# Mixing attention values on 64 x 64 diagonal blocks, with accumulators by query halves

## Time and profile before

| | |
|---|---|
| median of three runs | 1387.43 us |
| the profiled execution | 1390.95 us |
| its span | 1389.2 us |
| TensorE matmul busy | 1332.2 us |
| VectorE busy | 900.5 us |
| ScalarE busy | 754.5 us |
| POOL busy | 682.5 us |
| mean granted TensorE clock | 0.991 |

### The profile page before, as it was taken

The page is one execution under the profiler, slowest core; times in us unless marked ns, Lnnn a source line. Parts: engine busy times, 40 slices in busy tenths (PEclk is TensorE's granted clock), DMA queues, the critical chain, the costliest instruction groups (busy, mean ns, idle before and its releaser), DMA issues.

```text
span 1389.2 us, 34054 instructions
## 1 busy us (share of the span) xinstructions
PE 1332.2 (96%) x12776; PEld 1037.0 (75%) x12776; DVE 900.5 (65%) x1496; ACT 754.5 (54%) x2685; POOL 682.5 (49%) x719
## 2 busy tenths in 40 slices
PE   6798888999999999999999999999999999999998
PEld 3586666877778777777778777787777877777776
DVE  6657774477755777457764677547775577745775
ACT  2346664266733666256662666526663366624665
POOL 5226553266541766236652465426654176623664
PEclk9899999999999999999999999999999999999999
DMA  6214441424322342323414144142432234231332
GB/s 236 67 63 134 125 124 54 138 74 116 103 86 82 97 125 87 112 69 100 132 58 142 49 111 132 32 137 76 123 95 91 77 101 122 85 114 54 100 102 60
DMA packets 71554, 138.35 MB, mean 100 GB/s; under 512 B 15328, under 2 KB 29152, under 8 KB 71136
## 3 DMA queue, kind: packets, MB, share of 16 engines
q1 hardware_dynamic: 70400, 135.46, 33.7%
q10 hardware_dynamic: 992, 0.73, 0.2%
HBM read 73.21 MB, written 12.58 MB: 62 GB/s over the span
## 4 chain that ended last, share of the span: by engine, by line
PE 79%; DVE 7%; POOL 5%; ACT 5%; issue 3%; DMA 1%; SPq 0%; DVEq 0%; POOLq 0%
PE PROJ L898 14%; PE PROJ L899 13%; PE PROJ L900 13%; PE O L1072 13%; PE S L1042 11%; PE TR L1053 8%; ACT e_sb L596 2%; POOL e_sb L488 2%; PE S L898 2%; PE S L899 2%; PE S L900 2%; DVE S L822 1%; DVE negmax L829 1%; POOL p_cur L496 1%; PE S L982 1%
## 5 line engine op out<-in xcount | busy, mean ns | idle before, releaser
L596 ACT ACTIVATE e_sb<-S,negmax 128x128 f32<-128x128 f32 x1024 | 362.4, 369 | 127.4 <-DVE negmax L829 126.4
L488 POOL TENSOR_TENSOR e_sb<-e_sb,rinv 128x512 f32<-128x512 f32 x256 | 266.0, 1039 | 287.9 <-DVE rinv L834 262.6
L712 DVE TENSOR_TENSOR prod<-PROJ,rope_sb 128x1024 f32<-128x1024 f32 x160 | 195.5, 1222 | 86.4 <-PE PROJ L900 85.3
L1042 PEld LDWEIGHTS S<-k_stack,q_stack 64*64 64x64 f32 x5632 | 171.3, 133 | 72.0 <-issue 39.0
L822 DVE COPY_PREDICATED S<-diagonal_key,S 128x512 f32<-128x512 int8 x192 | 133.1, 693 | 124.4 <-PE S L1042 124.0
L1042 PE MATMUL S<-k_stack,q_stack 64*64 64x64 f32 (+2 forms) x5632 | 213.2, 275 | 0.0
L596 ACT ACTIVATION_READ_ACCUMULATOR e_sb<-S,negmax 128x1 f32 x1024 | 211.7, 207 | 0.0
L606 ACT ACTIVATE pt_sb<-TR 128x512 f32<-128x512 f32 x256 | 153.7, 600 | 91.1 <-PE TR L1053 87.9
L496 POOL TENSOR_SCALAR_AFFINE_SELECT p_cur<-pt_sb 128x512 f32<-128x512 f32 x256 | 163.2, 638 | 51.9 <-ACT pt_sb L606 46.6
L1053 PE MATMUL TR<-ident,e_sb 128*128 128x128 f32 x1024 | 167.6, 286 | 21.1 <-POOL e_sb L488 16.4
L829 DVE TENSOR_REDUCE negmax<-S 128x4 f32<-128x512 f32 x256 | 177.0, 691 | 8.8
(11 more groups left out here) (96 smaller groups left out, 2609.4 us busy)
## 6 DMA issues: line engine op xcount, KB each, us to landing
q_stack<-qy SPq DMA_DIRECT2D x512, 64.0 KB, 2.0
wq_ring<-wq_split_d SPq DMA_DIRECT2D x56, 512.0 KB, 3.5
wo_ring<-wo_split_d SPq DMA_DIRECT2D x56, 512.0 KB, 3.3
k_stack<-ky SPq DMA_DIRECT2D x256, 64.0 KB, 2.1
x_in<-x SPq DMA_DIRECT2D x8, 512.0 KB, 4.1
wq_split_d<-wq_ring SPq DMA_DIRECT2D x8, 512.0 KB, 3.7
wo_split_d<-wo_ring SPq DMA_DIRECT2D x8, 512.0 KB, 3.6
out<-acc SPq DMA_DIRECT2D x8, 512.0 KB, 4.9
```

Of the source, the lines that this page charges most:

```text
L488: nc.gpsimd.tensor_tensor(e, e, r, ALU.mult).then_inc(norm_done, 1)
L596: last = nc.scalar.activation(e_sb[:, n % 2, r, :], s_heads(n, 1)[:, r, :], ACT.Exp, bias=negmax[:, n % 2, r:r + 1], accum_out=rowsum[:, n ...
L712: nc.vector.tensor_tensor(prod[:, 2 * part:2 * part + 2, :], both, rope_sb[:, :, :], ALU.mult).then_inc(prod_done, 1)
L1042: last = nc.tensor.matmul(dst[:, at:at + (blocks - 1) * step + 1:step, :], q_stack[rows, g % 2, slot, i * P + a * HP:i * P + (a + 1) * HP] ...
```

## The change

The mixing works by halves of the 128 queries (a = 0 and 1). For queries of the first half, only places k < 64 can be of tile i; for those of the second half, places k < 64 always are, and only the others can be of either. So the first part of a step multiplies all of P (pt_sb, no longer p_cur) with v[i-1] for a = 0, and for a = 1 with v_mix, whose lower 64 places are of v[i] and upper 64 of v[i-1]. The second part multiplies only the diagonal 64 x 64 blocks of p_cur with v_step, on 64 rows. For i = 0 the scores' own mask already made P right, so neither mask nor second part is needed.

Half a = 0 accumulates in O, half a = 1 in the first half of TR, the transposes' bank. So the mixing of a pair waits for the copy of the transposes made in the same slot, and the transposes of odd slots wait (tr_read) until VectorE has read the half in TR. They are moved behind the filler of their slot. ScalarE and VectorE read the accumulators in two instructions, the half in TR first, and VectorE does so ahead of the fold. VectorE builds v_mix by `value_mix` in slots 0, 2 and 4. The load of Silu's table moves from slot 31 to slot 34.

```diff
+        O_half = [O[:, 0:2 * P].rearrange("p (s m q) -> p s m q", s=2, m=2),
+                  TR[:, 0:2, :].rearrange("p s (m q) -> p s m q", m=2)]
...
-                    if n >= 2:
+                    if 2 <= n <= STEPS + 1 and (n - 2) % TT:
                         mask(n - 2)
...
                     act.wait_ge(pv_done, b * STEPS + 2 * pair + 2)
-                    nc.scalar.activation(o_p[0][:, :, i * P:(i + 2) * P],
-                                         O[:, :].rearrange("p (m q) -> p m q", m=2), ACT.Copy
-                                         ).then_inc(o_copied, 1)
+                    for a in (1, 0):
+                        nc.scalar.activation(o_half(0, i, a), O_half[a].rearrange("p s m q -> p m s q"), ACT.Copy
+                                             ).then_inc(o_copied, 1)
...
-                    if n == STEPS - 1 and b + 1 < BATCH:
+                    if n == LAST_SLOT and b + 1 < BATCH:
                         load_table(ACT.Silu)
...
-                dve.wait_ge(o_copied, (row * STEPS) // 2 + pair + 1)
-                low(o_p[1][:, :, i * P:(i + 2) * P], O[:, :].rearrange("p (m q) -> p m q", m=2),
-                    o_p[0][:, :, i * P:(i + 2) * P]).then_inc(o_split, 1)
+                for a, done in ((1, tr_read), (0, o_split)):
+                    dve.wait_ge(o_copied, row * STEPS + 2 * pair + 2 - a)
+                    low(o_half(1, i, a), O_half[a].rearrange("p s m q -> p m s q"), o_half(0, i, a)).then_inc(done, 1)
...
+                def value_mix(i):
+                    dve.wait_ge(v_done, b * TT + i + 1)
+                    HP = P // 2
+                    nc.vector.tensor_copy(v_mix[0:HP, i - 1, :], v_sb[0:HP, i, :])
+                    nc.vector.tensor_copy(v_mix[HP:P, i - 1, :], v_sb[HP:P, i - 1, :]).then_inc(v_mixed, 1)
...
                 for n in range(LAST_SLOT + 1):
-                    early = n % 2
-                    if 1 <= n <= STEPS and early:
-                        inverse_sum(n - 1)
-                    if n < STEPS:
-                        fold(n)
-                    if 1 <= n <= STEPS and not early:
+                    if 1 <= n <= STEPS and n % 2:
                         inverse_sum(n - 1)
                     if n >= 5 and n % 2:
                         o_low(b, (n - 5) // 2)
+                    if n < STEPS:
+                        fold(n)
+                    if 1 <= n <= STEPS and n % 2 == 0:
+                        inverse_sum(n - 1)
+                    if n in (0, 2, 4):
+                        value_mix(1 + n // 2)
...
                         pe.wait_ge(t_copied, b * STEPS + n)
+                    if n >= 3 and n % 2:
+                        pe.wait_ge(tr_read, (b * STEPS + n - 3) // 2 + 1)
...
+                def values_mixed(pair):
+                    HP = P // 2
+                    pe.wait_ge(t_copied, b * STEPS + min(2 * pair + 3, STEPS))
+                    pe.wait_ge(v_done, b * TT + min(2 * pair + 2, TT))
+                    pe.wait_ge(v_mixed, b * (TT - 1) + min(2 * pair + 1, TT - 1))
+                    if pair:
+                        pe.wait_ge(o_split, b * STEPS // 2 + pair)
+                    for s in range(2):
+                        g, i = divmod(2 * pair + s, TT)
+                        heads = slice(g * D, (g + 1) * D)
+                        for a in range(2):
+                            v = v_mix[:, i - 1, heads] if i and a else v_sb[:, max(i - 1, 0), heads]
+                            for odd in range(2):
+                                last = nc.tensor.matmul(O_half[a][odd * D:(odd + 1) * D, s, :, :], v,
+                                                        pt_sb[:, (2 * pair + s) % 4, odd:REP:2, a * HP:(a + 1) * HP],
+                                                        start=s == 0, stop=False)
+                    pe.wait_ge(v_stepped, b * (TT - 1) + min(2 * pair + 1, TT - 1))
+                    for s in range(2):
...
+                        if i:
+                            pe.wait_ge(p_masked, b * MASKS + masks_upto(2 * pair + s))
+                            for odd in range(2):
+                                for a in range(2):
+                                    half = slice(a * HP, (a + 1) * HP)
+                                    last = nc.tensor.matmul(O_half[a][odd * D:(odd + 1) * D, s, :, :],
+                                                            v_step[half, i - 1, heads], p_cur[half, (2 * pair + s) % 4, odd:REP:2, half],
+                                                            start=False, stop=s == 1)
+                    last.then_inc(pv_done, 2)
...
-                    if 2 <= n <= STEPS + 1:
+                    if 2 <= n <= STEPS + 1 and n % 2 == 0:
                         transposes(n - 2)
...
+                    if 2 <= n <= STEPS + 1 and n % 2:
+                        transposes(n - 2)
                     if n >= 4 and n % 2 == 0:
-                        values_mixed(n - 4)
-                        values_mixed(n - 3)
+                        values_mixed((n - 4) // 2)
```

More of the change, by code:

```diff
@@ L122, in place, with masks_upto @@
         return TURN[what] % 2, TURN[what] + 1
+    def masks_upto(n):
+        return n - n // TT
+    MASKS = masks_upto(STEPS - 1)
     def stacked(b, g, semaphores, each):
@@ L176, in attention_and_ffn_block @@
         v_step = sb("v_step", [P, TT - 1, NKV * D])
-        staging_rest = sb("staging_rest", [P, CT * 2 * F - (TT - 1) * NKV * D])
+        v_mix = sb("v_mix", [P, TT - 1, NKV * D])
+        staging_rest = sb("staging_rest", [P, CT * 2 * F - 2 * (TT - 1) * NKV * D])
         qy = sb("qy", [P, 2, 2, T])
@@ L205, in attention_and_ffn_block, with o_half @@
         O = ctx.enter_context(nc.psum_tensor("O", [P, 512], fp32))
+        O_half = [O[:, 0:2 * P].rearrange("p (s m q) -> p s m q", s=2, m=2),
+                  TR[:, 0:2, :].rearrange("p s (m q) -> p s m q", m=2)]
         PROJ = ctx.enter_context(nc.psum_tensor("PROJ", [P, 2, 512], fp32))
         S4 = S[:, :, :, :, :].rearrange("p a b h k -> p (a b) (h k)")
+        def o_half(part, i, a):
+            tokens = o_p[part][:, :, i * P:(i + 2) * P].rearrange("p m (s a q) -> p m s a q", s=2, a=2)
+            return tokens[:, :, :, a, :]
         def s_heads(n, which):
@@ L278, in attention_and_ffn_block @@
         v_stepped = sem("v_stepped")
+        v_mixed = sem("v_mixed")
         pv_done = sem("pv_done")
@@ L281, in attention_and_ffn_block @@
         o_split = sem("o_split")
+        tr_read = sem("tr_read")
         wo_added = sem("wo_added")
@@ L513, in _ @@
                 rotate(b, "q", 2)
-                for n in range(STEPS + 2):
+                for n in range(LAST_SLOT + 2):
                     if 1 <= n <= STEPS:
@@ L1054, in transposes @@
                     last.then_inc(t_ready, 1)
[L1056 to L1072, removed]
-                                                    v[:, g * D:(g + 1) * D], p[:, n % 4, odd:REP:2, :],
-                                                    start=term == 0, stop=term == len(terms) - 1)
-                    last.then_inc(pv_done, 1)
+                def values_mixed(pair):
[16 more added lines that the diff above has]
+                    for s in range(2):
+                        g, i = divmod(2 * pair + s, TT)
+                        heads = slice(g * D, (g + 1) * D)
+                        if i:
[7 more added lines that the diff above has]
+                    last.then_inc(pv_done, 2)
```

## The result

The changed kernel takes 1397.46 us (median of five runs, 1395.18 to 1400.03) against 1387.43 (1386.48 to 1390.48) of the kernel before on the same chip: ratio 1.0066, 95% interval 1.0044 to 1.0088. It is slower, by 0.66%; the forecast was 1389.7, no change. One execution in experiment 11, the profiled one, took 2551 us where the others took 1379; it is left out, and no rows of it are used.

What follows compares the result with a forecast made beforehand. TensorE, busy 96% of the span, was taken as the bound. Six middle rows -3.9, last row +4.1 and first row +2.1 made +2.3 on the profiled 1390.95; with the median 3.5 lower, 1389.7 us, range 1376 to 1403.

Steps and rivals of the forecast that it cites:

- part 1: Mixing on TensorE: cheaper products save 0.43 us per pair of steps with i > 0, 0.21 with i = 0.
- the rival of 1431: Each TensorE instruction has its own price, 0.36 to 0.48 us more a pair, giving 1431 us; chance 0.03.
- Five switches before, five after: TensorE's changes of tile shape, 0.16 us each, stay equal in number per pair; bounds 0 to +0.16, taken as 0.
- part 2: Even slots' transposes wait for ScalarE's copy of the odd slot's: 0.05 us lost for i > 0, 0.26 for i = 0.
- thin cover of 0.13: In even slots the Q block hides mixing's wait for ScalarE's copy of the transposes by only 0.13 us.
- ScalarE's second copy: Rival: mixing is held by ScalarE's copy of the even slot's transposes; 0.25 us later adds 14 us, 1404; chance 0.22.
- The 1397 that this rival gives: Half of the +14 us for a late ScalarE copy, with value_mix calls of 1.36 us (+6), was said to give 1397.
- part 3: VectorE's value_mix, three calls a row: 0.80 to 1.36 us each, taken as 0.85; slots 1 to 6 net -0.1 a row.
- part 4: Places lacking cover: slot 24 +1.1 a row, pair (30, 31) gains nothing, last row +4.1, first row +2.1 us.
- Six such slots at 0.6: First row: waits behind weight splits lose 1.6 us each where about 1.0 before; with three lesser slots, +4 us.
- the saving arrives: Rival: a quarter to a half of the products' 41 us saving is kept, giving 1369 to 1380; chance of faster 0.29.
- plain wait of 0.95 against 0.69: Even slots, i = 0: ScalarE's copy frees the transposes after 0.95 us, while TensorE would be there at 0.69.

Runs made afterwards that it cites:

- experiment 11: The kernel before, with ScalarE's weight-split halves ahead of the exponentials and odd slots' transposes in the middle of the odd filler; ratio 0.9925.
- experiment 4: The changed kernel with the odd slots' transposes moved from behind the filler block to its middle; 1382.38 us, ratio 0.9952.
- experiment 1: The kernel before with only the odd slots' transposes moved behind the filler block, mixing, masks and accumulators untouched; 1410.12 us, ratio 1.0155.
- experiment 3: The changed kernel without value_mix, reading v_sb in place of v_mix (wrong values, same products); 1387.45 us, ratio 0.9995.
- experiments 9 and 10: Kernel before and changed kernel, each with ScalarE's halves of the first row's weight splits issued early, ahead of the exponentials; 1374.03 and 1377.46 us.

## Why the forecast was right or wrong

*Products (part 1): right.* 30 us left TensorE's busy time. Without the wait (experiment 4) a pair gains 0.39 and 0.15 against the forecast's 0.43 and 0.21. No price of an instruction shows: the rival of 1431 is dead. By the page "TensorEngine Tiling (Array Packing)" of the Trainium skill (Performance Considerations) the added matmuls would have taken back an estimated 0.3 to 0.4 a pair, if its overhead comes on top of each one's columns; the pairs disagree, with 0.04 and 0.06 missing. "Five switches before, five after" held within the same 0.04 to 0.06.

*The new wait (part 2): right.* Pairs of 7.14 and 6.91 against 7.13 and 6.91, 56 waits with 0.18 at i = 0, and experiment 1 shows the same wait without the products. Mixing's thin cover of 0.13 held: no wait of it in slots 16 to 19, so the rival "ScalarE's second copy" did not happen there: a steady row has two such waits, in slot 24 and at its end. The first row has ten (3.4 us). The 1397 that this rival gives with slow copies of the values is a wrong sum (1389.7 + 7 + 6 is 1403), and that the result lies beside it is chance. The read of TR was covered by 1.2 us, as worked out (1.1 against 2.2).

*value_mix (part 3): mis-sized.* "I take 0.85" a call; it measures 0.573 + 0.809 = 1.38 in the mean, just above the upper bound of 1.36, since half of its passes run beside POOL's. Its cost is 1.15 a row by removal (experiment 3), not the 0.2 that the sum held. The value was chosen by the look of a row with one tensor read, and not by what POOL does in those slots. A second error hides most of the first: with the copies gone, slots 0 to 7 take 23.92, 0.97 less than in the kernel before, where the forecast had 0.33. It is not the order (experiment 1 has 24.95 there). The traces point at the masks that POOL no longer makes for i = 0, which the forecast priced at nothing: in experiment 1, with the new order and all masks, a mask of 0.63 stands ahead of the scaling for slot 4, which starts 10.2 after the row's first scores, and that slot's mixing waits 0.42 for POOL's p_cur; in experiment 3 the scaling starts at 9.6, and there is no such wait. No run leaves out the masks alone, so this is a reading. The two leave +0.29 instead of -0.1, and rows 2 to 7 at -1.6 instead of -3.9. By the page "VectorE: DVE Perf Modes" of the Trainium skill (Mode 2x_2P) a call was an estimated 0.86; its 0.43 a copy agrees with the 0.41 of a copy beside an idle POOL, and the mean does not.

*Slot 24, row's end and last row (part 4): right in kind.* Slot 24 +0.92 (forecast +1.1); the pair (30, 31) +0.11 with the row's end (forecast 0); the last row's late pairs +3.9 (+3.8) and its end +1.8 (+1.7), the whole row +4.8 (+4.1, the rest is the row's start again).

*First row (part 4): the step that failed in the medians.* "Six such slots at 0.6" was read from one stall of a profiled execution that was itself a long one of before. The profiled pair shows +0.8, but with 10.2 us of the first row at the lower clock before and 6.8 after. The medians differ by 10.0. Less the stages that repeat in the profiled executions (-1.6 and +4.8), 6.8 are left for the first row and the ends, where the forecast had 2.1; and with the early split the medians differ by 3.4 only. The forecast put the granted clock at nothing. It was 0.991 in the changed kernel's median execution, and the median of before lies among those at 0.994: 0.003 of 1390 us is 4 us, an estimate of the clock's part in the 10.0. That the first row has these 6.8 us in the median run is worked out from experiments 9 and 10 and seen in no trace, since only one execution of each was profiled.

Together: 4.7 in the first row and the ends, 2.3 in rows 2 to 7 and 0.7 in the last are the 7.7 of 7.8 us between forecast and result. The rival "the saving arrives" is what experiment 4 built by moving the transposes; in the kernel as changed the plain wait of 0.95 against 0.69 stood against it, as argued. The direction was undecided in the forecast (0.37 slower, 0.34 same), and what tipped it was a term paid once a row, and the first row's stalls, whose cause (ScalarE's order) was there before, with the clock that goes with them. The range of 1376 to 1403 held the time, with two errors of opposite sign inside it.

## What to carry to other kernels

When a cheaper product brings a new wait, look for the position in the queue at which both ends of the wait are covered; here the middle of a block was worth 1.3%, its end or its start a loss. Cost a small pass on VectorE by what POOL does at that moment, not by its size. And look at the stage that differs from the rest (the first row, 21 us longer than the others): moving ScalarE's work ahead of four exponentials gave the kernel before more (1.2%) than the change under study could. Before comparing two profiled executions, compare the clock that each was granted.

## What the runs showed of the hardware

- Passes over SBUF of VectorE and POOL slow each other: a 64x512 fp32 copy took 0.41 us alone and up to 1.19 beside POOL, a two-input pass of the same size 0.67 alone and up to 1.44; POOL's 128x512 pass went from 1.28 to a mean of 1.35 and 1.43, up to 1.74. The products of VectorE that read one input from PSUM (`prod`, 1.22 beside `v_step` too) did not show it, nor did ScalarE's copies (0.63).
- Cutting products in two had next to no price of its own: the mixing of a pair takes 1.51 us with 32 matmul records of 128 columns, and took 1.88 with 16 of 256; 1.28 of columns and a fixed 0.16 are 1.44, so at most 0.07 is left for 16 more records.
- An accumulator copy of 128x256 by ScalarE takes 0.38, against 0.60 for 128x512: two halves cost 0.16 more than the whole.
- The run-to-run spread of one kernel on one core goes with the granted clock: the kernel before took 1386.7 to 1388.0 us in 13 executions at 0.994 and 1389.9 to 1392.3 in 12 at 0.991. In the traces the lower level (1.2 GHz) shows in the first row, where TensorE stood still often (busy 43.3 of 50 us); with the stalls removed, the executions were at 0.996 and within 0.7 us.
